# Moving the start-up of a four-layer residual kernel: x tiles before adapter tables, layer 0 in three PSUM banks, four gate products before the last selections

## What is computed

```python
x = x + einsum('bct,bcd->bdt', x, w0[subject]) + bias[subject][:, :, None]
g = x @ Wg + (x @ Ag[i]) @ Bg[i];  u = x @ Wu + (x @ Au[i]) @ Bu[i]
h = silu(g) * u
x = x + h @ Wd + (h @ Ad[i]) @ Bd[i]
x = x + x @ W2.T + scal[j] * (x @ A2[j].T) @ B2[j].T
x = x + einsum('bct,bcd->bdt', x, w3[condition])
```

## Time and profile before

| | us |
|---|---|
| median of 3 runs | 761.57 (761.23 to 762.88) |
| the profiled execution, its own time | 756.74 |
| its span | 754.9 |
| TensorE busy | 719.9 (95%) |
| TensorE weight loads busy (beside it) | 610.6 (81%) |
| VectorE busy | 583.3 (77%) |
| ScalarE busy | 286.8 (38%) |
| GpSimd busy | 261.7 (35%) |

### The profile page before, as it was taken

The page is one execution under the profiler, slowest core; times in us unless marked ns, Lnnn a source line. Parts: engine busy times, 40 slices in busy tenths (PEclk is TensorE's granted clock), DMA queues, the critical chain, the costliest instruction groups (busy, mean ns, idle before and its releaser), DMA issues.

```text
span 754.9 us, 10625 instructions
## 1 busy us (share of the span) xinstructions
PE 719.9 (95%) x3666; PEld 610.6 (81%) x3666; DVE 583.3 (77%) x979; ACT 286.8 (38%) x502; POOL 261.7 (35%) x489
## 2 busy tenths in 40 slices
PE   8598889999999999998899999999999999899997
PEld 7576678888888888877778888888888888788885
DVE  5966868797878788789988879797978796864542
ACT  1445423333424243343353433333424242434444
POOL 3933641415233232342237161616253331222100
PEclk9799999999999999999999999999999999999999
DMA  6486321213212121413712222322222043201112
GB/s 155 141 140 201 116 74 35 99 45 103 82 58 84 56 84 56 84 29 112 246 61 94 68 93 70 105 65 88 81 66 85 29 131 93 83 29 51 63 56 83
DMA packets 80725, 66.02 MB, mean 87 GB/s; under 512 B 42912, under 2 KB 65440, under 8 KB 80672
## 3 DMA queue, kind: packets, MB, share of 16 engines
q1 hardware_dynamic: 73056, 45.92, 20.7%
q0 software_dynamic: 7296, 19.41, 8.4%
q10 hardware_dynamic: 320, 0.02, 0.0%
HBM read 56.94 MB, written 8.39 MB: 87 GB/s over the span
## 4 chain that ended last, share of the span: by engine, by line
PE 79%; DVE 9%; issue 6%; DMA 2%; ACT 2%; POOL 1%; SPq 0%; POOLq 0%; DVEq 0%; ACTq 0%
PE bank L1394 34%; PE bank L1494 21%; PE bank L1402 7%; PE bank L1634 5%; PE bank L1504 4%; PE bank L1623 2%; PE bank L1651 2%; DMA BR<-in_L_cond_Bu_dram,boffs 1%; PE bank L1610 1%; PE bank L1640 1%; PE bank L1347 1%; DMA adsel<-in_L_cond_weights_dram 1%; DVE hid L1040 1%; DVE hs L1046 1%; PE bank L1371 1%
## 5 line engine op out<-in xcount | busy, mean ns | idle before, releaser
L1394 PE MATMUL bank<-XC,WC 128*128 128x512 f32 x1344 | 331.8, 393 | 10.6 <-DVE tmp L1014 3.7
L1394 PEld LDWEIGHTS bank<-XC,WC 128*128 128x128 f32 x1344 | 244.0, 189 | 58.2 <-DVE tmp L1014 4.1
L1494 PE MATMUL bank<-hs,wds 128*128 128x512 f32 x768 | 186.3, 391 | 8.0 <-DVE wds L999 4.1
L1494 PEld LDWEIGHTS bank<-hs,wds 128*128 128x128 f32 x768 | 141.8, 188 | 37.2 <-DVE wds L999 4.6
L421 POOL DMA_INDIRECT BR<-in_L_cond_Bu_dram,boffs x64 | 70.7, 1104 | 258.6 <-DVE BL L993 244.0
L421 POOL DMA_INDIRECT BR<-in_L_cond_Bg_dram,boffs x64 | 76.1, 1189 | 92.7 <-DVE BL L993 77.0
L638 ACT ACTIVATE hs<-hid 128x512 fp32r<-128x512 f32 x64 | 40.3, 630 | 168.1 <-DVE hid L1040 112.9
L1057 DVE TENSOR_TENSOR XA<-bank,XA 128x512 f32<-128x512 f32 x128 | 86.4, 686 | 18.4 <-PE bank L1494 14.8
L632 ACT ACTIVATE hid<-hid 128x512 f32<-128x512 f32 x48 | 30.4, 633 | 152.1 <-issue 60.4
L1402 PEld LDWEIGHTS bank<-UT,BL 128*128 128x128 f32 x512 | 76.4, 189 | 10.8 <-issue 2.1
L1402 PE MATMUL bank<-UT,BL 128*128 128x256 f32 x512 | 81.8, 282 | 1.6 <-DVE hid L1037 1.3
(11 more groups left out here) (164 smaller groups left out, 809.5 us busy)
## 6 DMA issues: line engine op xcount, KB each, us to landing
RW<-in_L_cond_Wg_dram SPq DMA_DIRECT2D x16, 512.0 KB
RW<-in_L_cond_Wu_dram SPq DMA_DIRECT2D x16, 512.0 KB
RD<-in_L_cond_Wd_dram SPq DMA_DIRECT2D x16, 512.0 KB
out_dram<-XB SPq DMA_DIRECT2D x16, 256.0 KB, 2.1
XB<-in_x_dram SPq DMA_DIRECT2D x8, 256.0 KB, 7.3
x1park<-XB SPq DMA_DIRECT2D x8, 256.0 KB
x2park<-XA SPq DMA_DIRECT2D x8, 256.0 KB, 2.7
XA<-x1park SPq DMA_DIRECT2D x4, 512.0 KB
```

What stands on the lines that cost most here:

```text
L1394: last = nc.tensor.matmul(psum[:, :], WC[:, t, left, a, k, :], XC[:, right, b, k, :], start=(first and k == 0 and n == 0), stop=(k == 1 an ...
L1494: last = nc.tensor.matmul(psD[j % 2][:, :], by_feature(wds[:, f, a, :])[:, j % KT, :], hs[:, f, b, j // KT * 512:(j // KT + 1) * 512], sta ...
```

## The change

It touches the head up to unit 1 and leaves the arithmetic as it is.

- **Loads (SyncE).** x tiles 3 to 11 stand ahead of the two A tables; tiles 12 to 15 stand right behind them, no longer between the loads of Ad. The parking of pairs 8 to 15 stands behind the load of unit 2's gate weights.
- **GpSimd.** Layer 0's matrices of pairs 8 to 13 are placed before the A columns are selected, those of pairs 14 and 15 after it.
- **Banks.** Layer 0 uses three banks, and so `layer0(p)` waits for pair p-3 to be copied, not for p-4. The second adapter result and the odd selections use bank R1 in the first half, so that bank C is free for P5.
- **TensorE.** P1, P6 and P5 stand between the layer-0 tiles, ahead of all selections; A12 x B21 stands ahead of selections 2 and 3. The waits for UT that P5 had are now at the adapter rows.
- **VectorE and ScalarE.** The head's lists follow: the bias table's second half and the move matrices come first, the x combinations ahead of the adapters' splits. `p_combine(0)` (the sums of unit 0's up weights) comes before the last selections are read.
- **Unit 1.** VectorE does `sum_u3` and `sum_half22` ahead of `sums_low`, and in the slot with two sets of down products the evictions ahead of `hs_low(1, 0, 0)` except the last.

```diff
         def l0_bank(p):
-            return (psD[0], psD[1], psR[0], psR[1])[p % 4]
+            return (psD[0], psD[1], psR[0])[p % 3]
+        def u_bank(h, m):
+            return (psE, (psR[1], psC)[h])[m % 2]
...
-                for p in range(3, 6):
+                for p in range(3, HP):
                     load_x(p)
+                for p in range(HP, HP + XIN):
+                    load_xin(p)
                 load_a(0)
-                load_x(6)
-                load_x(7)
-                for p in range(HP, HP + XIN):
+                for p in range(HP + XIN, PAIRS):
                     load_xin(p)
...
-                for p in range(HP, PAIRS):
-                    park_x1(p)
                 load_u(1)
...
                         load_g(unit + 2)
+                    if unit == 0:
+                        for p in range(HP, PAIRS):
+                            park_x1(p)
...
-                for q in range(HQ):
-                    select_a(0, q, cols)
...
+                for p in range(HP + 4, PAIRS):
+                    if p == PAIRS - 2:
+                        for q in range(HQ):
+                            select_a(0, q, cols)
+                    place_w0(p, late[2 * (p - HP):2 * (p - HP) + 2])
...
-                    if p >= 4:
-                        pe.wait_ge(s_xr, p - 3)
+                    if p >= 3:
+                        pe.wait_ge(s_xr, p - 2)
...
+                def first_gate_products():
+                    pe.wait_ge(s_xcl, filled(0, B11))
+                    pe.wait_ge(s_wr[G], 1)
+                    p1_product(0, G)
+                    layer0(HP + 2)
+                    layer0(HP + 3)
+                    pe.wait_ge(s_wl[G], 1)
+                    pe.wait_ge(s_xcl, filled(0, T2))
+                    p6_product(0, G)
+                    adapters_in(0, 0)
+                    layer0(HP + 4)
+                    layer0(HP + 5)
+                    pe.wait_ge(s_xcl, filled(0, T1))
+                    p5_product(0, G)
+                    adapters_in(0, 1)
+                    select(0, 0)
+                    select(0, 1)
+                    layer0(HP + 6)
+                    layer0(HP + 7)
...
                     product(psA, t, A12, B21, False)
+                    if n == 0:
+                        pe.wait_ge(s_um, 1)
+                        select(0, 2)
+                        select(0, 3)
                     pe.wait_ge(s_bl, 2 * b + 1)
...
                 for p in range(3):
                     xr_sum(p)
                 g_combine(0)
                 xr_sum(3)
-                biases(1)
+                raw_low(G, 0)
                 xr_sum(4)
-                raw_low(G, 0)
                 xr_sum(5)
-                move_matrices()
+                masks()
                 xc_low(0, B11)
                 xr_sum(6)
+                xr_sum(7)
+                t3_sum(0)
                 xc_low(0, B21)
-                xr_sum(7)
-                masks()
+                t2_sum(0)
+                xc_low(0, B22)
+                xc_low(0, T3)
                 sums_low(G, 0)
+                t1_sum(0)
+                xc_low(0, T2)
                 a_low(0, 0)
                 a_low(0, 1)
-                t3_sum(0)
-                xc_low(0, B22)
                 a_sum(0)
-                xc_low(0, T3)
+                t4_sum(0)
+                xc_low(0, T1)
                 a_low(0, 2)
                 a_low(0, 3)
-                t2_sum(0)
+                xc_low(0, T4)
                 u_low(0, 0)
-                xc_low(0, T2)
-                t1_sum(0)
+                p_combine(0)
                 u_low(0, 1)
...
-                    w_low(U, unit)
+                    raw_low(U, unit)
+                    if unit == 1:
+                        sum_u3(n)
+                        sum_half22(n, tmp[:, 3, :], 1)
+                    sums_low(U, unit)
...
-                    hs_low(unit, 0, 0, 1)
+                    if len(slots[2]) < 2:
+                        hs_low(unit, 0, 0, 1)
                     evicts(unit, slots[2], 0)
+                    if len(slots[2]) == 2:
+                        hs_low(unit, 0, 0, 1)
                     evicts(unit, slots[2], 1)
```

More of the change, by code:

```diff
@@ L464, in _ @@
                         place_w0(p, cols[2 * p:2 * p + 2])
-                for q in range(HQ):
-                    select_a(0, q, cols)
-                for g in range(2, 4):
-                    late = adapters(8 * g, 8)
-                    for p in range(4 * g, 4 * g + 4):
-                        place_w0(p, late[2 * (p - 4 * g):2 * (p - 4 * g) + 2])
+                late = adapters(16, 8)
+                for p in range(HP, HP + 4):
+                    place_w0(p, late[2 * (p - HP):2 * (p - HP) + 2])
+                late += adapters(24, 8)
+                for p in range(HP + 4, PAIRS):
+                    if p == PAIRS - 2:
+                        for q in range(HQ):
+                            select_a(0, q, cols)
+                    place_w0(p, late[2 * (p - HP):2 * (p - HP) + 2])
                 pool.wait_ge(s_boffs, 1)
@@ L641, in gate_window @@
                     n, i = 2 * unit, unit % UNITS
-                    p1_copy(n)
+                    if unit:
+                        p1_copy(n)
                     if i:
@@ L689, in _ @@
                 sums_high(G, 0)
+                xc_high(0, B22)
+                xc_high(0, T3)
+                xr_copy(HP)
+                xc_high(0, T2)
+                xr_copy(HP + 1)
                 a_high(0, 0)
                 a_high(0, 1)
[L692 to L693 removed]
+                xc_high(0, T1)
+                xr_copy(HP + 2)
+                xr_copy(HP + 3)
                 a_high(0, 2)
+                xc_high(0, T4)
                 a_high(0, 3)
                 u_high(0, 0)
[L697 to L699 removed]
+                xr_copy(HP + 4)
+                xr_copy(HP + 5)
+                p1_copy(0)
                 u_high(0, 1)
[L701 to L705 removed]
                 b_high(0, 0)
[L707 removed]
                 xr_copy(HP + 6)
@@ L1087, in gate_window @@
                         gated(unit - 1, n - 1, 1, 4, 4)
-                    p_combine(unit)
+                    if unit:
+                        p_combine(unit)
                     sum_u2(n)
@@ L1093, in gate_window @@
                     b_low(2 * unit, 1)
-                    w_low(U, unit)
+                    raw_low(U, unit)
[3 more added lines that the diff above has]
+                    sums_low(U, unit)
                     if i:
                         ad_low(unit - 1)
-                    sum_u3(n)
-                    sum_half22(n, tmp[:, 3, :], 1)
+                    if unit != 1:
+                        sum_u3(n)
+                        sum_half22(n, tmp[:, 3, :], 1)
                     evicts(unit, slots[0], 0)
@@ L1199, in _ @@
                 u_own(0, 3)
-                xc_low(0, T4)
                 for unit in range(ALL):
@@ L1524, in gate_and_up @@
                         p5_product(n, G)
-                    else:
-                        first_gate_products(unit)
-                    if unit == 0:
-                        layer0(HP + 6)
-                        layer0(HP + 7)
+                    elif unit:
+                        second_half_products(unit)
+                    else:
+                        first_gate_products()
                     c11_product(n, G, 2 * unit)
```

63 lines of the change are left out of this document (17 added, 46 removed).

## The result

The kernel after takes 747.74 us (median of 4 runs, 747.51 to 749.29), the kernel before beside it 761.4 (755.76 to 762.88). The ratio is 0.984, with an interval of 0.980 to 0.988. The profiled execution took 747.92 on its own clock with a span of 746.1. That is 8.8 less than the 756.74 before, where I had forecast 7.0.

The account below looks back on a forecast made before the run. TensorE bounds the kernel, busy 719.9 of 754.9 us. Leads of 4.8 and 2.2 sum to 7.0, taking the profiled 756.74 to 749.7; plus 4.8 from profile to median gives 754.6, range 752.2 to 758.0.

Parts of the forecast that it names:

- Up to P6 at 34.3: Head, set by VectorE: bias sums end by 20.7, then masks 1.2, two sums 1.2, nine operations 11.2; P6 starts at 34.3.
- Three banks at no cost: Layer-0 tiles in the head: one micro-wait of 1.1 lies within an idle stretch that ends at 34.3 anyway.
- From P6 to A22 x T4 in 26.4: Unit 0: 19.5 of steps plus 2.0 for the clock, then 0.7 and 4.2; A22 x T4 at 60.7, 2.2 earlier.
- the 2.0 for the clock: Head: after idleness as long as before, P6 and part of the adapter group run at 1.2 GHz, losing 2.0.
- GpSimd covered: Head: twelve additions end at 29.5, the A-column selection of 6.75 at 36.2, in time for both adapter groups.
- Rival 1: GpSimd becomes the bound: twelve additions at 1.24, first adapter group at 39.9, cost 2.7, time 757.3; chance 0.15.
- From unit 0 to unit 1, 2.6 more: Up to unit 1's A22 x T4: gated product's wait of 1.1 goes, `sum_u3` saves 1.7; lead grows from 2.2 to 4.8.
- The down product, 2.2 more: Down product at 112.13: with the split behind three evictions, the eviction wait of 2.2 goes whole.
- The sum of the profile, 749.7: Whole profiled execution: 7.0 less than 756.74 gives 749.7.
- From the profile to the median, plus 4.8: Whole kernel: the median of 761.57 was 4.8 above the profiled execution; carrying that difference gives 754.6.
- Rival 2: Head: the clock holds as TensorE is busy from 20.5 to 30; the 2.0 are won, 752.6; chance 0.12.
- Rivals 3, 4 and 5: Parkings hit unit 1's gate gather, 756.1, 0.08; clock stays low, 766.6, 0.05; stalls return, 761.6, 0.05.

Follow-up runs that it names:

- c_before: The kernel before, unchanged, profiled and timed again: median 756.99 us.
- e_unit1: The kernel before with only unit 1's VectorE orders: `sum_u3` and `sum_half22` ahead of `sums_low`, three evictions ahead of `hs_low`; 754.16 us, ratio 0.9937.
- a_bcast: The kernel after with the two small DMAs (indices, scalings) put back ahead of the bias copies: 749.28 us.
- c_after: The kernel after, unchanged, profiled and timed again: median 747.53 us, ratio 0.986 to the kernel before.
- e_bcast_unit1: The kernel before with the bias copies moved ahead of the two small DMAs and unit 1's new VectorE orders: 751.15 us.
- a_noparks: The kernel after with the eight parkings back ahead of the load of unit 1's up weights: 748.66 us.
- v_order: The kernel after with x combinations reordered and P6, P5 and pairs 12 and 13 ahead of both adapter groups: 747.99 us.
- e_loads: The kernel before with only x tiles 3 to 11 loaded ahead of the A tables: 760.28 us, ratio 1.0025.

## Why the forecast was right in its parts and wrong in its sum

**Up to P6 at 34.3: right for the kernel that I added up, 2.5 late for this one.** From the end of the sixth bias sum on, the masks took 1.6 and not 1.2, and the sums and splits 1.2 each. What failed is the first number, "the fifth and sixth bias sums end by 20.7": they ended at 17.8. I took the head's start as given. The edit was in the change, as one line, `bias_copies()`, that stood two lines higher in ScalarE's list; the sum put what it did to the DMAs behind it at nothing. **This is the missing term:** -1.8 in time, up to -4 in the lead.

**Three banks at no cost: right.** The one wait of a layer-0 tile between 20 and 31 us, 1.57 for a bias sum at 21.34, stands for my 1.1, and 4.50 of idleness stand behind it.

**From P6 to A22 x T4 in 26.4: right within 1.0.** It took 25.41 (25.96 and 26.42 in the other two). Of the 2.0 for the clock 1.2 to 2.2 were lost; the granted clock is at 0.50 (1.2 GHz) from 31.3 to 34.7, behind 4.50 of idleness, and back at 1.00 soon after the adapter group starts. `sum_u3` bound the selections' end as said: 1.15 of wait ahead of 57.20.

**The reason for the 2.0 was misread, and its size is partly luck.** The forecast says that 4.10 of idleness had cost the clock before. But that idleness runs from 26.5 to 30.6, and the clock had fallen ahead of it, at 25.6, in the middle of P1:

```profile
25.00:26.00 1.00, 1.00 (x5) 0.67 (x4) 1.00 (x2) 0.00 (x0) 1.00 (x2) 0.78 0.00 0
```

In c_before it fell still earlier, at 21.7, while layer-0 tiles ran. What stood ahead of the fall in these two were waits of 1.9 to 2.4 us between 18 and 25. A long idle stretch behind the fall can't have caused it, and what does set the moment stays open.

**GpSimd covered: right, with another price.** The additions of the second half got shorter, and the selection got longer: it now runs beside eight of VectorE's operations on 1024 columns, where two ran beside it before. GpSimd's groups by line up to 45 us, before and after: busy us, mean ns.

```profile
L442 POOL COPY tmp<-RW 128x128 f32 x16 | 6.7, 469 | 0.2 <-POOL hid L409 0.2
...
L409 POOL TENSOR_TENSOR w0second<-adsel,ident 64x64 f32<-64x64 f32 x16 | 11.2, 701 | 1.3 <-POOL tmp L442 0.3
```

```profile
L442 POOL COPY tmp<-RW 128x128 f32 x16 | 12.5, 829 | 0.2 <-POOL w0second L409 0.2
L409 POOL TENSOR_TENSOR w0second<-adsel,ident 64x64 f32<-64x64 f32 x16 | 7.8, 486 | 2.0 <-issue 1.0 <-POOL tmp L442 0.2
```

A copy of 128 x 128 took 469 ns before and 829 now, beside VectorE's splits with two SBUF inputs; 6.75 became 12.47 for the sixteen. The Trainium skill, SBUF — State Buffer, section "SBUF: two separate sides", has the shared lock for VectorE with two SBUF inputs and a GpSimd operation that reads SBUF, and these rows fit it. Rival 1 put the price on the additions, which fell from 701 to 486. The cover held: VectorE waited 1.37 for the copies at 34.64, and P6 did not depend on them.

**From unit 0 to unit 1, 2.6 more: right.** 5.75 of lead became 8.30. The terms were 1.1 for the gated product and 1.74 for `sum_u3`'s place; e_unit1 has the second alone.

**The down product, 2.2 more: right.** 8.30 became 10.65, which is 2.35.

**The sum of the profile, 749.7:** the profiled execution took 747.92, a_bcast 749.28 in the median.

**From the profile to the median, plus 4.8: wrong, the largest error, and the step on which the forecast failed.** Of the 6.9 between 754.6 and 747.7, 4.8 are this step, 1.8 the two DMAs, and 0.3 the rest. The 4.8 were the difference between two groups of executions of the kernel before, by how long the clock was low, and the changed kernel has only the second one: its profiled execution took 747.92 and its median is 747.74, a difference of -0.2. In e_unit1 the orders of unit 1 alone went with the same; a_bcast, c_after and the variants keep it. But that these orders are the cause is not shown: e_bcast_unit1 has them too, and three of its six executions have 0.986, though at 751.5 to 752.5 they cost only about 1. In which part of the kernel the executions of the first group were at the low clock is open: no profile fell on one.

**Rival 2**, that the clock holds, came in part: the low stretch of the head is 3.4 us here and 6.8 in c_after, where it was 10.2 before, and it still cost 1.2 to 2.2. **Rivals 3, 4 and 5** did not come. a_noparks shows the parkings holding another gather than that of my third rival: at their old place it is that of unit 0's up rows, by 1.16; at their new place, beside unit 1's gate rows, ScalarE waits for none.

## What to carry to other kernels

Read the head from its first wait on, and for every DMA that a change moves, however small, ask who lands beside it: twenty kilobytes cost 1.8 us here. Give a profiled execution's difference, and carry a gap between profile and median only if the granted clocks of the runs say that the changed kernel will have it too; here it had not, and what removed the gap is open. When a head is won, look one gather further: v_order gave back 2.4 us to one late transfer, and moving four small loads into an idle stretch of the queue won 3.0 in the lead.

## What the runs showed of the hardware

- Two DMAs of 16 KB and 4 KB to all 128 partitions, issued at 2.09 and 2.56, moved the landing of 128 KB that had been issued at about 2.0 from 3.1 to 7.3 us after issue. GpSimd's first addition was at 9.4 to 9.9 in all four kernels in which they stood there, and at 5.6 to 6.2 in all eight in which they stood behind the bias copies. SyncE's issue of the 512 KB load at 4.25, 2.07 in the rows above, is no such mark: beside the two DMAs it took 0.43 in c_before, 0.54 in e_unit1, 0.97 in e_loads and 2.02 in a_bcast (without them 0.43 each time), and the additions started late in all of them. The Trainium skill, DMA: Bandwidth & Descriptors, section "Queues, rings and completion order", says that a DMA's completion is signalled only after every earlier write of the same DMA engine, from whatever queue. That would fit these rows; no run here tells it from plain sharing of the engines.
- The same 16 copies of GpSimd took 6.75 us beside two of VectorE's 1024-column operations and 12.47 beside eight; no run changed this alone. An addition of 64 x 64 took from 311 ns to 1207.
- One kernel's executions spread from 754.6 to 763.6 with the mean granted clock (0.995 to 0.982), in two groups whose medians are 4.8 apart.
- The granted clock fell at different moments in two executions of one kernel (25.6 and 21.7 before, 31.3 and 30.0 after), and behind the same 3.0 of idleness at the turn it fell in one and not in the other.
